# Gated experts with stationary input weights, copied a tile ahead, and 23 tiles written out

## Reference, cut to what matters

```python
def _L3_ffn_ref(hidden_states, router_w, gate_w, up_w, down_w):
    ...
    w, sel = jax.lax.top_k(probs, TOP_K)
    w = w / jnp.sum(w, axis=-1, keepdims=True)
    combine = combine.at[jnp.arange(T)[:, None], sel].add(w)

    def body(acc, ew):
        g, u, d, c = ew
        h = jax.nn.silu(x @ g) * (x @ u)
        return (acc + c[:, None] * (h @ d), None)
```

## Time and profile before

| | |
|---|---|
| time, median of 3 runs | 862.2 us (858.91 to 863.43) |
| the profiled execution's own time | 863.15 us |
| its span | 861.4 us |
| TensorE busy | 625.5 us (73%) |
| VectorE busy | 419.9 us (49%) |
| ScalarE busy | 289.5 us (34%) |
| GpSimd busy | 230.0 us (27%) |
| gated2, first to last transpose of slots | 478.0 to 548.3 us |
| gated3, first to last transpose of slots | 774.5 to 838.9 us |

### The profile page before, as it was taken

How to read it: one execution, slowest core, us unless ns; L and a number is a source line. 1 busy time by engine, 2 the same in 40 slices (tenths; PEclk the granted TensorE clock), 3 DMA queues, 4 the chain that set the end, 5 groups by cost and what they waited for, 6 DMA issues and landing times. The chain is left out here.

```text
span 861.4 us, 14476 instructions
## 1 busy us (share of the span) xinstructions
PE 625.5 (73%) x4568; PEld 474.8 (55%) x4569; DVE 419.9 (49%) x1096; ACT 289.5 (34%) x826; POOL 230.0 (27%) x275
## 2 busy tenths in 40 slices
PE   4888679775199999927963799833977999528771
PEld 2556566455189999913652366511544666414441
DVE  3674456783633333265956233247644453352333
ACT  1285223772044444303420233320631444202220
POOL 2033010132145553110000466303400111115651
PEclk9999899898589999967965899955886999757996
DMA  7970000000110010018500111010000000001122
GB/s 230 356 290 1 1 0 1 2 1 7 38 30 26 25 24 18 13 56 320 172 0 25 34 41 41 27 49 2 1 0 2 2 2 2 5 27 40 43 40 85
DMA packets 28984, 44.77 MB, mean 52 GB/s; under 512 B 5458, under 2 KB 18402, under 8 KB 28674
## 3 DMA queue, kind: packets, MB, share of 16 engines
q1 hardware_dynamic: 24514, 35.02, 12.2%
q0 software_dynamic: 4416, 9.05, 4.1%
HBM read 37.44 MB, written 6.62 MB: 51 GB/s over the span
## 5 line engine op out<-in xcount | busy, mean ns | idle before, releaser
L1105 PE MATMUL experts_ps<-experts_act,experts_own 128*128 128x128 f32 x736 | 86.0, 275 | 0.2 <-ACT experts_act L1160 0.2
L1285 PE MATMUL gated_ps_in<-experts_w_in,gated_slots_t 128*128 x138 | 75.5, 659 | 13.4 <-issue 5.7
L1105 PEld LDWEIGHTS experts_ps<-experts_act,experts_own 128*128 128x128 f32 x736 | 84.0, 192 | 0.3 <-issue 0.3
L1160 ACT ACTIVATE experts_act<-experts_ps,experts_b 128x128 f32<-128x128 f32 x184 | 52.6, 369 | 72.1 <-PE experts_ps L1105 57.4
L1038 POOL DMA_INDIRECT gated_slots<-ffn_tokens,keep_ffn_token x46 | 44.6, 969 | 72.8 <-issue 46.6
L1196 DVE COPY experts_own<-experts_w 128x2048 f32 x23 | 28.2, 1226 | 64.5 <-PE experts_ps L1105 64.5
L642 POOL TENSOR_TENSOR core_e<-core_e,core_inverse 128x1024 f32<-128x1024 f32 x16 | 30.4, 1902 | 103.6 <-DVE core_inverse L787 103.6
L1029 POOL DMA_INDIRECT ffn_results<-gated_results,keep_ffn_row x46 | 45.4, 986 | 37.6 <-DVE gated_results L1381 28.7
L1038 POOL DMA_INDIRECT experts_slots<-ffn_tokens,keep_ffn_token x23 | 36.8, 1599 | 63.1 <-PE experts_ps L1086 41.2
L1371 DVE COPY gated_slots_t<-gated_ps_x 128x128 f32<-128x128 f32 x46 | 13.4, 292 | 82.5 <-PE gated_ps_x L1277 72.3
L1304 PEld LDWEIGHTS gated_ps_y<-experts_w_out,gated_gated_t 128*128 128x128 f32 x276 | 35.9, 197 | 24.4 <-issue 24.4
(11 more groups left out here) (390 smaller groups left out, 1372.6 us busy)
## 6 DMA issues: line engine op xcount, KB each, us to landing
experts_w<-in_L_ffn_W SPq DMA_DIRECT2D x1, 8192.0 KB, 40.2
experts_w_in<-in_gated_in SPq DMA_DIRECT2D x1, 4096.0 KB, 12.3
combine_mine<-ffn_results SPq DMA_DIRECT2D x12, 256.0 KB, 3.5
experts_w<-in_L_ffn_W SPq DMA_DIRECT2D x1, 2048.0 KB, 11.6
experts_w_out<-in_gated_out SPq DMA_DIRECT2D x1, 2048.0 KB, 17.2
ffn_tokens<-route_xn SPq DMA_DIRECT2D x3, 512.0 KB, 3.2
experts_w_in<-in_L_ffn_gate_w SPq DMA_DIRECT2D x1, 1024.0 KB, 7.6
experts_w_in<-in_L_ffn_up_w SPq DMA_DIRECT2D x1, 1024.0 KB, 10.4
```

The source lines that it names most:

```text
L1105: mm = pe.matmul(ps_2[u][:, c * P:(c + 1) * P], own2[:, u, k, c * P:(c + 1) * P], act1[:, u, k, :], start=(k == 0), stop=(k == chunks - 1))
L1160: act.activation(to[:, u, c, :], source[u][:, c * P:(c + 1) * P], ACT.Gelu, bias=bias[:, bass.ds(e * chunks + c, 1)]).then_inc(done, 1)
L1285: mm = pe.matmul(ps_in[:, banks * u + n], slots_t[:, u, :], w_in[:, bass.ds(e, 1), 512 * n:512 * n + 512].rearrange("d a h -> d (a h)"), s ...
```

## The change

`up` swaps its operands. The stationary operand is now a 128-column chunk of the expert's input weights and the moving operand is the turned slots. The result has hidden units on the partitions, so that `down` can use the gated values as they are: `turn`, `ps_t`, `gated_t` and `keep_gated` go. Because the stationary operand has a fixed address, ScalarE copies the expert's 2 x width columns into `own` (two buffers), up to two tiles ahead of their use, after the silu of tile j for tile j + 2. TensorE loads the expert's number for `down` only. The loops of the three engines are replaced by 23 tiles written out. GpSimd's part (`move_tiles`) stays as it is. The orders within a tile change too, as the diff shows.

```diff
-        gated, gated_t = s.sb("gated", [P, 2, width]), s.sb("gated_t", [P, 2, chunks, P])
+        own, gated = s.sb("own", [P, 2, 2 * chunks, P]), s.sb("gated", [P, 2, chunks, P])
-        ps_in = s.psum("ps_in", [P, 2 * banks, 512])
-        ps_x, ps_t, ps_y = s.psum("ps_x", [P, 512]), s.psum("ps_t", [P, 512]), s.psum("ps_y", [P, 512])
+        ps_in = s.psum("ps_in", [P, 2, banks * 512])
+        ps_x, ps_y = s.psum("ps_x", [P, 512]), s.psum("ps_y", [P, 512])
...
             @block.tensor
             def _(pe):
+                def turn_slots(j):
+                    if j >= TILES:
+                        return
+                    u = j % AHEAD
+                    pe.wait_ge(keep.gathered[u], 16 * (j // AHEAD + 1) + routes.gathers_before[u])
+                    if j:
                         pe.wait_ge(sem["slots_kept"], j)
                     pe.transpose(ps_x[:, 0:P], slots[:, u, :], keep.identity[:]).then_inc(sem["turned"], 1)
 
-                def up(j, u, first=False):
-                    e = expert_index(pe, routes, j)
+                def up(j):
+                    if j >= TILES:
+                        return
                     pe.wait_ge(sem["slots_kept"], j + 1)
-                    if not first:
+                    pe.wait_ge(sem["own_kept"], j + 1)
+                    if j >= 2:
                         pe.wait_ge(sem["gated_ready"], j - 1)
-                    for n in range(banks):
-                        mm = pe.matmul(ps_in[:, banks * u + n], slots_t[:, u, :],
-                                       w_in[:, bass.ds(e, 1), 512 * n:512 * n + 512].rearrange("d a h -> d (a h)"),
+                    for c in range(2 * chunks):
+                        mm = pe.matmul(ps_in[:, j % 2, c * P:(c + 1) * P], own[:, j % 2, c, :], slots_t[:, j % 2, :],
                                        start=True, stop=True)
                     mm.then_inc(sem["in_made"], 1)
 
-                def turn(j, u, first=False):
...
-                def down(j, u, first=False):
-                    e = expert_index(pe, routes, j)
-                    pe.wait_ge(sem["gated_kept"], j + 1)
+                def down(j):
+                    e = expert_index(pe, routes, j)
+                    pe.wait_ge(sem["gated_ready"], j + 1)
+                    if j:
                         pe.wait_ge(sem["result_kept"], j)
                     for c in range(chunks):
-                        mm = pe.matmul(ps_y[:, 0:D], gated_t[:, u, c, :],
+                        mm = pe.matmul(ps_y[:, 0:D], gated[:, j % 2, c, :],
...
+                turn_slots(0)
+                up(0)
+                turn_slots(1)
+                turn_slots(2)
+                for j in range(TILES):
+                    up(j + 1)
+                    if j:
+                        turn_slots(j + 2)
+                    down(j)
 
             @block.scalar
             def _(act):
+                def own_weights(j):
+                    if j >= TILES:
+                        return
+                    e = expert_index(act, routes, j)
+                    if j >= 2:
+                        act.wait_ge(sem["in_made"], j - 1)
+                    act.activation(own[:, j % 2].rearrange("d c h -> d (c h)"),
+                                   w_in[:, bass.ds(e, 1), :].rearrange("d a h -> d (a h)"), ACT.Copy)\
+                        .then_inc(sem["own_kept"], 1)
+
+                def silu(j):
                     act.wait_ge(sem["in_made"], j + 1)
+                    if j >= 2:
                         act.wait_ge(sem["result_made"], j - 1)
+                    act.activation(gated[:, j % 2].rearrange("p c k -> p (c k)"), ps_in[:, j % 2, 0:width], ACT.Silu)\
+                        .then_inc(sem["silu_done"], 1)
+
+                act.wait_ge(loaded, loads)
+                own_weights(0)
+                own_weights(1)
+                for j in range(TILES):
+                    silu(j)
+                    own_weights(j + 2)
 
             @block.vector
             def _(dve):
...
+                keep_slots(0)
+                keep_slots(1)
+                multiply(0)
+                keep_slots(2)
+                for j in range(1, TILES):
+                    multiply(j)
+                    keep_slots(j + 2)
+                    keep_result(j - 1)
+                keep_result(TILES - 1)
```

More of the change, by code:

```diff
@@ L1309, in _ @@
                 pe.wait_ge(loaded, loads)
[L1310 to L1321, removed]
-                        turn_ahead(turn_slots, i, v)[u]()
-                        down(j - 1, u, first and u == 0)
-                        turn(j, 1 - u)
@@ L1326, in _ @@
-                steady(0, 0, True)
-                steady(0, 1)
-                with pe.Fori(1, (TILES - 3) // 4) as i:
-                    for v in range(2):
-                        steady(i, v)
-                j = TILES - 2
-                up(j + 1, 0)
-                down(j - 1, 0)
-                turn(j, 1)
-                down(j, 1)
-                turn(j + 1, 0)
-                down(j + 1, 0)
+                turn_slots(0)
+                up(0)
+                turn_slots(1)
+                turn_slots(2)
@@ L1358, in _ @@
-                keep_gated(1, 1, True)
-                with act.Fori(0, (TILES - 3) // 2) as i:
-                    for u in range(2):
-                        silu(3 + 2 * i + u, 1 - u)
-                        keep_gated(2 + 2 * i + u, u)
-                keep_gated(TILES - 1, 0)
+                def own_weights(j):
[7 more added lines that the diff above has]
+                        .then_inc(sem["own_kept"], 1)
@@ L1379, in keep_result @@
+                def keep_result(j):
                     dve.wait_ge(sem["result_made"], j + 1)
-                    wait_scattered(dve, keep, routes, u, round)
-                    dve.tensor_copy(results[:, u, :], ps_y[:, 0:D]).then_inc(sem["result_kept"], 1)
-                keep_slots(0, 0, True)
-                keep_slots(1, 1, True)
-                multiply(0, 0)
-                multiply(1, 1)
-                keep_slots(2, 0)
-                def steady(i):
-                    for n in range(AHEAD):
-                        j = AHEAD * i + 1 + n
-                        keep_slots(j + 2, 1 - n % 2)
-                        multiply(j + 1, n % 2)
-                        keep_result(j - 1, n, i)
@@ L1396, in _ @@
-                steady(0)
-                with dve.Fori(1, (TILES - 3) // AHEAD) as i:
-                    steady(i)
-                j = TILES - 2
-                multiply(j + 1, 0)
-                for n in range(j - 1, TILES):
-                    keep_result(n, n % AHEAD, n // AHEAD)
+                    wait_scattered(dve, keep, routes, j % AHEAD, j // AHEAD)
+                    dve.tensor_copy(results[:, j % AHEAD, :], ps_y[:, 0:D]).then_inc(sem["result_kept"], 1)
+                keep_slots(0)
```

53 lines of the change are left out of this document (10 added, 43 removed).

## The result

The changed kernel takes **869.6 us** (median of 7 runs, 866.45 to 873.65) against 862.2: a ratio of 1.0086, 95% interval 1.0058 to 1.0115. It is slower. The profiled execution took 869.58 us with a span of 867.8, which is 6.4 us more than the span of before.

What follows compares the result with a forecast made beforehand. It took gated2 as bound by TensorE's issue order and gated3 as mixed (GpSimd's indirect DMAs, late signals). gated2 +7.2, gated3 -4.6 and unrolling 0 gave +2.6 us on 863.15, or 864.8 on the median; range 856 to 871.5.

Steps and rivals of the forecast that it cites:

- The likeliest case: Whole kernel: the forecast as summed, 864.8 us, with gated2 slower and gated3 faster; chance 0.47.
- What bounds the kernel before: gated2: TensorE's issue order, 3.16 us a tile; gated3: mixed, GpSimd's indirect DMAs at least 2.57, late signals some 7.3 us.
- Parts 1 and 2: TensorE: dropping the turn saves 0.44 us a gated2 tile, `up` with stationary weights adds 0.07; alone 2.79 us a tile.
- Part 3: ScalarE's copy of the expert's weights, 1.064 us a tile, is covered and costs nothing.
- Part 4: Serial chain: `down` waits on T's slots copy, then the result copy; 0.94 us from T, gated2 3.70 a tile, +7.2 us.
- Part 5: gated3: 2.37 us a tile undisturbed; stage -11.9 to -4.6 us, taken as -4.6 with late signals staying.
- my signs of being wrong: Trace: gated2 tile under 3.2 us, `down` 0.11 after T, `up` awaiting the weight copy, or TensorE half clock mid-stage.
- Part 6: Writing out the loops removes branches and register arithmetic: taken as 0, bounds -7.3 to +2 us.
- The first rival: gated3's late signals vanish with the loops: stage -11.9 us, time 857.5 us; chance 0.23.
- The second rival: Late signals come wherever TensorE runs dry, so in gated2 too: up to 877.8 us; chance 0.15, in full or part.
- the rival's other half: gated2: 12% of the time at half clock, costing about 3.2 us, within the 877.8 us price.
- The third rival: `down`'s serial waits don't bind: gated2 2.79 us a tile, gated3 2.57, time 843.7 us; chance 0.07.

Runs made afterwards that it cites:

- E7: Changed kernel with the two waits ahead of `down` exchanged, so that result_kept comes last; 874.2 us, ratio 1.0152 to the kernel before.
- E6: The changed kernel run again, unedited, beside the kernel before; 873.4 us, ratio 1.0127.
- E2: Changed kernel with two PSUM buffers for `down`'s result instead of one, VectorE's order untouched; 837.1 us, ratio 0.9775 to the kernel before.
- E3: Kernel before with only the loops of gated2 and gated3 written out; 851.3 us, ratio 0.9968 to the kernel before.
- E1: Changed kernel with two VectorE instructions exchanged, keeping result j-1 ahead of slots j+2; 838.8 us, ratio 0.9787 to the kernel before.
- E8: Changed kernel with ScalarE's weight copy made twice a tile, first into an unread spare buffer; 875.7 us, ratio 1.0134 to the kernel before.
- E10: Changed kernel with two buffers for `down`'s result and ScalarE's weight copy made twice; 850.8 us, ratio 0.9859 to the kernel before.
- E5: The kernel before run again, unchanged, for its trace; 862.2 us, ratio 1.0004.
- E12: Kernel before with the loops of gated2 and gated3 written out, run again on another chip; 860.7 us, ratio 0.9978.
- E9: Changed kernel with two buffers for `down`'s result and VectorE keeping result j-1 ahead of slots j+2; 851.7 us, ratio 0.9861 to the kernel before.
- E11: Changed kernel with gated3's gathers on GpSimd replaced by plain SyncE loads of consecutive rows; 858.4 us, ratio 0.9949 to the kernel before.

## Why the prediction held, and where its terms were off

The time forecast, 864.8 us, was 4.8 too low; 869.6 lies inside the range of 856.0 to 871.5. Of the 4.8 us, 3.1 are gated2's, 0.9 gated3's, 0.95 came from putting the forecast on the median (this time the profiled execution is the median), and the rest of the program takes 0.2 off. That the rest came out so near is luck, as the 2.0 and 1.8 us above show; in E7's trace it is 3.7 us shorter than in E6's. Of the three outcomes it was "slower by over 0.5%", to which I had given 0.31 and not the most: the interval of the ratio begins at 1.0058. The likeliest case was the one that happened, with gated2's cost taken too small and gated3's gain too large.

*What bounds the kernel before.* Right for gated2. For gated3 I took GpSimd's 2.57 us a tile as a lower bound, which is wrong over 18 tiles: TensorE enters with a lead of gathers and uses it up. In E2 GpSimd starts 15 pairs of indirect DMAs without a break from 772.28 to 810.80 us, 2.57 us a pair, but the tiles from T3 to T10 take 1.65 us each and those from T10 to T22 2.62. In all E2 took 41.4 us from T4 to T22, 2.30 a tile, and E3 40.5 us, 2.25.

*Parts 1 and 2.* Right. `up` has 1.79 us against 1.78 forecast, and the tile without the chain is 2.789 against 2.79 (E1, E2).

*Part 3, the copy costs nothing.* Right: 1.057 us against 1.064, and doubled it still costs nothing in a tile of 3.82 us (E8) or of 2.79 (E10).

*Part 4, the chain.* The mechanism is right, one link too short. I took 0.14 us from the result copy's end to `down`'s weight load, from the earlier trace rows, where the awaited signal was the last wait before the load. Here a second wait stands behind it and the link is 0.24 (532.64 to 532.88). 0.10 us over 19 tiles is 1.9 us, and E7 brings exactly this link back to 0.14 (532.24 to 532.38). The rest of the tile was 0.02 long (`up` and `down` 0.01 each), 0.4 us. The start was 0.5 us longer than forecast (T0 to T3 9.96 us against 10.36 before, -0.4 where I had -0.9; E1, E2 and E7 show 9.4 to 9.6), the end 0.3 longer. Together +10.3 instead of +7.2.

*Part 5, gated3.* The sum was near (-3.7 against -4.6), its terms less so. The undisturbed tile is 2.48 us against 2.37, again by the 0.10 link. T4 came 1.5 us earlier after T0 than forecast, T4 to T22 gave 0.7 us instead of 2.9, the end 1.5 instead of 1.7. The late signals stayed, as I took it: 7.1 us of late copies where I had 7.3, though at other tiles and more even, so that the nearness of the two sums is in part luck. What I had no term for is the clock. TensorE at half clock in the middle of a stage stood among my signs of being wrong; the first trace doesn't show it (1.00 from 792 to 851 us), those of E6 (0.50 from 817 to 829), E7 (0.62 to 0.84) and E8 (0.79) do. In E6 gated3 took 72.7 us, which is 1.9 more than E5's 70.8 on the same chip, so that there the change gains nothing in gated3. That fits the larger ratio of that set.

*Part 6, unrolling.* I took 0 with a lower bound of -7.3. The runs give 2 to 3 us less (E3, E12), by the intervals 0 to 5. The instruction queues moved more, as the DMA queues of the changed kernel in 774 to 850 us show (packets, MB, share of 16 engines), three packets each for the one of the earlier trace rows. Written out, gated2 keeps the loops' 3.158 us a tile (E3, E12), so no engine that sets its pace was held up:

```profile
q8 instruction: 3, 0.05, 0.3%
q14 instruction: 3, 0.02, 0.1%
```

*The first rival, late signals go with the loops* (0.23): wrong. They are in the changed kernel, which has no loops there, and in E12. By the ratios of E3 and E12 writing the loops out gives 0.3% and 0.2%.

*The second rival, late signals wherever TensorE runs dry* (0.15): wrong as stated. TensorE idles 0.77 us in each tile of the changed gated2, with no late copy and a clock of 1.00. Where they did come into gated2, in E9, TensorE's tile had lost its idle time. But the rival's other half, the clock, was real in gated3 (0.50 in the 12 us of E6 above).

*The third rival, the chain doesn't bind* (0.07): wrong for this kernel, and its price of 843.7 us was near for the kernel without the chain. E1's and E2's ratios, applied to 862.2, are 843.8 and 842.8 us. On the chip with many late signals, E9's and E10's give 850. The nearness is in part luck, since the price rests on the 2.57 us a tile in gated3 that E1 and E2 undercut.

*What stays open.* What holds the signals back. The runs narrow it. In gated2 and gated3 late copies were seen where GpSimd's two indirect DMAs, 2.57 us, fill the tile or nearly do (2.48 us in the changed gated3, 2.79 in E9's gated2), and none where the tile is 3.16 or 3.82 us. On the chip of E1 to E3, gated2's tiles of 2.79 us show none (E1, E2), and gated3 two over 1 us in E1 and none in E2 and E3. With the gathers taken away, on a chip that shows them in three other kernels, there are none (E11). And their number differs from chip to chip for the same kernel (E3, E12). E9 and E10 ran on another chip than E1 and E2, so I can't say what E9 and E2 would differ by on one. Whether the signal or the last passes themselves are held can't be read either, since the ends of matmuls are modelled.

## What to carry to other kernels

When a change moves work from one engine's queue to another's, write the two queues side by side and follow each single-buffered tile: a wait one tile nearer than before, behind an instruction that itself waits for the newest result, turned a gain of 1.4 to 2.2% into a loss of 1% here, and either a second buffer or an exchange of two lines brought it back (E2, E1). Price a wake-up by a row in which the late wait stands where yours will, as the last or with another behind it (0.14 and 0.24 us here). And before trusting the difference of one stage between two traces, look whether the same kernel gives it twice, on the same chip.

## What the runs showed of the hardware

- Of the two waits ahead of `down` on TensorE, the place of the late one mattered: 0.24 us from the result copy's end to the weight load when the other wait follows it (E6), 0.14 when it is the last (E7).
- TensorE's clock fell in the middle of a stage though no idle time was longer than 2 us: in E6 TensorE's idle times between 792 and the fall at 816 us are of 0.8 to 1.9 us. At the lower level, 0.50, a tile of gated3 takes 3.91 us in place of 2.48. Why the first trace of the changed kernel kept 1.00 with much the same idle times (0.8 to 2.1 us) isn't settled.
- Signals of TensorE arrived 1 to 3.5 us late (0.97 in the changed kernel, 3.47 in E12), in E9 together for three groups of matmuls, and in gated2 and gated3 only in traces in which GpSimd's two indirect DMAs, 2.57 us, fill the tile or nearly do. E2 and E3 have such tiles in gated3 without a late signal. One and the same kernel took 59.5 us for a stage without them and 69.0 with them, on two chips (E3, E12).
- GpSimd's indirect DMAs started 1.28 us apart on average in gated3 of E2, where they followed each other without a break, but this set the pace of the stage only after the lead of gathers was used up: seven tiles of 1.65 us, then twelve of 2.62 on average, 2.30 over the 18 from T4 on.
